# Cross-attention with absorbed queries: remainders one step later, and another order of the prologue

## What is computed

```python
x = x + xattn(layernorm(x), ctx_768, Wq, Wk, Wv, Wo, bo)   # 16 heads of 64, no mask
x = x + attn(layernorm(x), wq, wk, wv, wo)                 # causal, 16 heads of 64
x = x + ffn(layernorm(x), router, gate, up, down)          # 8 experts, top 2, silu
```

```python
q = layernorm(x) @ Wq;  k = ctx @ Wk;  v = ctx @ Wv
out = softmax(q @ k.T * 64 ** -0.5) @ v;  x + concat(out) @ Wo + bo
```

## Time and profile before

| | us |
|---|---|
| median of 3 runs | 2505.78 (2503.46 to 2507.37) |
| the profiled execution | 2506.52 |
| its span | 2504.8 |
| PE busy in the span | 2282.4 (91%) |
| DVE busy | 1612.8 (64%) |
| ACT busy | 1273.0 (51%) |
| POOL busy | 833.2 (33%) |

### The profile page before, as it was taken

How to read it: one execution, slowest core, us unless ns; L and a number is a source line. 1 busy time by engine, 2 the same in 40 slices (tenths; PEclk the granted TensorE clock), 3 DMA queues, 4 the chain that set the end, 5 groups by cost and what they waited for, 6 DMA issues and landing times. The chain is left out here.

```text
span 2504.8 us, 56060 instructions
## 1 busy us (share of the span) xinstructions
PE 2282.4 (91%) x18992; PEld 2030.0 (81%) x18992; DVE 1612.8 (64%) x3655; ACT 1273.0 (51%) x3906; POOL 833.2 (33%) x1022
## 2 busy tenths in 40 slices
PE   6999999999999999989999699999999984999996
PEld 6878888888788878878888589999999972788885
DVE  5656655665666666656655488988988857444442
ACT  4444444444444444444444377667666641444442
POOL 2323322332232323232322222222222230677674
PEclk8999999999999999999999899999999985999998
DMA  3000000000000000000000400000000011333434
GB/s 99 26 18 11 23 17 25 8 25 17 25 8 25 17 25 8 25 17 13 21 13 5 144 1 19 17 8 17 17 8 17 18 43 32 97 77 76 102 52 101
DMA packets 61946, 82.52 MB, mean 33 GB/s; under 512 B 9936, under 2 KB 45520, under 8 KB 61808
## 3 DMA queue, kind: packets, MB, share of 16 engines
q1 hardware_dynamic: 48912, 63.46, 7.9%
q0 software_dynamic: 12960, 18.12, 4.3%
HBM read 59.80 MB, written 25.96 MB: 34 GB/s over the span
## 5 line engine op out<-in xcount | busy, mean ns | idle before, releaser
L401 POOL TENSOR_TENSOR p_sb<-p_sb,rinv 128x512 f32<-128x512 f32 x256 | 266.8, 1042 | 933.6 <-DVE rinv L741 933.6
L652 ACT ACTIVATE p_sb<-s_ps,nmax 128x256 f32<-128x256 f32 x512 | 238.4, 471 | 603.1 <-DVE nmax L724 566.2
L907 POOL TENSOR_TENSOR sp_sb<-sp_sb,srinv 128x512 f32<-128x512 f32 x128 | 133.4, 1042 | 424.9 <-DVE srinv L1101 424.9
L58 DVE SCALAR_TENSOR_TENSOR q_sb<-m_ps,q_sb 64x256 fp32r<-64x256 f32 x256 | 108.1, 422 | 218.3 <-ACT q_sb L46 216.4
L65 PE MATMUL s_ps<-cx_hi,qk_hi 128*128 128x256 f32 x512 | 170.1, 332 | 41.5 <-DVE qk_hi L57 39.2
L1049 ACT ACTIVATE sp_sb<-sm_sb,snmax 128x128 f32<-128x128 f32 x512 | 199.4, 390 | 7.2 <-DVE snmax L1112 4.1
L724 DVE TENSOR_REDUCE nmax<-s_ps 128x2 f32<-128x512 f32 x256 | 175.1, 684 | 30.7 <-PE s_ps L65 30.3
L45 ACT CAST qk_hi<-qk_ps 128x512 fp32r<-128x512 f32 x248 | 148.0, 597 | 75.9 <-PE qk_ps L65 75.9
L57 DVE TENSOR_TENSOR qk_lo<-qk_ps,qk_hi 128x256 fp32r<-128x256 f32 x248 | 105.4, 425 | 121.5 <-ACT qk_hi L45 116.8
L749 DVE COPY pt_sb<-t_ps 128x512 f32<-128x512 f32 x256 | 177.0, 691 | 8.3 <-PE t_ps L544 0.8
L544 PE MATMUL t_ps<-ident,p_sb 128*128 128x128 f32 x1024 | 156.0, 275 | 7.7 <-DVE pt_sb L749 2.3
(11 more groups left out here) (293 smaller groups left out, 7644.2 us busy)
## 6 DMA issues: line engine op xcount, KB each, us to landing
ctx_raw<-in_ctx_t SPq DMA_DIRECT2D x32, 256.0 KB, 2.8
ctx_raw<-in_ctx_t SPq DMA_DIRECT2D x64, 128.0 KB, 2.9
x_ring<-in_x SPq DMA_DIRECT2D x16, 256.0 KB, 2.8
x_mid<-x_ring SPq DMA_DIRECT2D x16, 256.0 KB, 2.2
xn<-f_xn SPq DMA_DIRECT2D x16, 256.0 KB, 2.2
acc<-x_sb SPq DMA_DIRECT2D x16, 256.0 KB, 2.3
e_raw<-in_gate SPq DMA_DIRECT2D x8, 512.0 KB, 3.9
e_raw<-in_up SPq DMA_DIRECT2D x8, 512.0 KB, 4.9
```

What stands on the lines that cost most here:

```text
L58: return nc.vector.scalar_tensor_tensor(out=lo, in0=src, scalar=scale, in1=f32(hi), op0=ALU.mult, op1=ALU.subtract)
L401: nc.gpsimd.tensor_tensor(prob, prob, inv, ALU.mult).then_inc(norm_done, 1)
L652: ex = nc.scalar.activation(p_sb[:, k, b * J:(b + 1) * J], s_ps[1 - w][:, b * J:(b + 1) * J], ACT.Exp, bias=nmax[:, k, b:b + 1], scale=1.0 ...
L907: nc.gpsimd.tensor_tensor(prob, prob, inv, ALU.mult).then_inc(norm_done, 1)
```

## The change

The units and projections of the middle groups are dealt out anew. In the odd tile step 1 and step 3 now have an early and a late unit, so that units 0 to 8 are made there, and 9 to 15 in steps 0 to 6 of the even tile; step 7 of the even tile has none. Projections go to steps 0, 1, 2, 4, 6 of the odd tile and 0, 2, 4 of the even one. The remainder of a late unit is no longer taken in its own step but in the next one, right behind the maximum. ACT rounds the projection (and in the first tile the late unit and the turned keys) ahead of the exponentials. DVE copies `pt_sb` ahead of the reciprocal. In the prologue five pairs of keys are turned ahead of the split of Wq instead of two behind it on ACT and DVE, and the identity products have 16 moving columns instead of 64.

```diff
-            EARLY_WK, WARM = 3, 24
+            EARLY_WK, WARM = 5, 24
+            ODD_PROJ, EVEN_PROJ = {0: 0, 1: 1, 2: 2, 4: 3, 6: 4}, {0: 5, 2: 6, 4: 7}
+            ODD_UNIT = {(1, False): 0, (1, True): 1, (2, True): 2, (3, False): 3, (3, True): 4,
+                        (4, True): 5, (5, True): 6, (6, True): 7, (7, True): 8}
...
-                if u == 1 and p % 2 == 0 and look:
-                    return PAIRS * (t // 2 + 1) + p // 2, p // 2
-                if u == 0 and p % 2 == 0 and not drain:
-                    return PAIRS * (t // 2) + PAIRS // 2 + p // 2, PAIRS // 2 + p // 2
+                if u == 1 and look and p in ODD_PROJ:
+                    return PAIRS * (t // 2 + 1) + ODD_PROJ[p], ODD_PROJ[p]
+                if u == 0 and not drain and p in EVEN_PROJ:
+                    return PAIRS * (t // 2) + EVEN_PROJ[p], EVEN_PROJ[p]
...
             def absorption(t, u, p, first, look, drain, late):
-                m = PAIRS * (t // 2)
                 if first:
                     return p, p, int(late), 0
-                if u == 1 and p and late and look:
-                    pair = (p - 1) // 2
-                    return m + PAIRS + pair, pair, (p - 1) % 2, PAIRS * t + 1 + pair
-                if u == 0 and not drain and (late or p == PAIRS - 1):
-                    i = PAIRS - 1 + p + (p == PAIRS - 1 and late)
-                    return m + i // 2, i // 2, i % 2, PAIRS * t - PAIRS + 1 + i // 2
+                if u == 1 and look and (p, late) in ODD_UNIT:
+                    i = ODD_UNIT[p, late]
+                    return PAIRS * (t // 2 + 1) + i // 2, i // 2, i % 2, PAIRS * t + 1 + i // 2
+                if u == 0 and not drain and late and p < PAIRS - 1:
+                    i = PAIRS + 1 + p
+                    return PAIRS * (t // 2) + i // 2, i // 2, i % 2, PAIRS * t - PAIRS + 1 + i // 2
                 return None
+
+            def unit_behind(t, u, p, first, look, drain):
+                if first or drain:
+                    return None
+                if p:
+                    return absorption(t, u, p - 1, False, look, False, True)
+                return absorption(t - 1, 1, PAIRS - 1, False, True, False, True) if u == 0 else None
...
# PE, prologue
-                    pe.matmul(y_ps[:, 0:HEAD], ident[:], ident[:, 0:HEAD], start=True, stop=True)
+                    pe.matmul(y_ps[:, 0:16], ident[:], ident[:, 0:16], start=True, stop=True)
...
# ACT, tile: these lines now stand ahead of the exponentials instead of behind them
+                        if first:
+                            absorbed_hi(*late, two_banks=True)
+                            if EARLY_WK + p < PAIRS:
+                                wk_hi_copy(EARLY_WK + p)
+                        if proj is not None:
+                            q_hi(*proj)
...
# ACT and DVE, prologue: wk_hi_copy and wk_lo_copy of pairs 1 and up ahead of the split of Wq
+                for pair in range(1, EARLY_WK):
+                    wk_hi_copy(pair)
                 for n in range(Q_SPLIT):
                     weights.split_hi(act, n)
-                for pair in range(1, EARLY_WK):
-                    wk_hi_copy(pair)
...
# DVE, tile
+                        behind = unit_behind(t, u, p, first, look, drain)
...
                             (maximum)
+                        if behind is not None:
+                            absorbed_lo(*behind[:3], two_banks=False)
...
-                        if (not first if p < LAG_S else cur):
-                            dve.wait_ge(exp_done, n)
-                            nc.vector.reciprocal(rinv[:, (p - 1) % 4, :], rsum[:, (p - 1) % 4, :]).then_inc(rinv_done, 1)
-                        if late is not None and not first:
-                            absorbed_lo(*late[:3], two_banks=False)
...
                             (copy of pt_sb)
+                        if (not first if p < LAG_S else cur):
+                            dve.wait_ge(exp_done, n)
+                            nc.vector.reciprocal(rinv[:, (p - 1) % 4, :], rsum[:, (p - 1) % 4, :]).then_inc(rinv_done, 1)
```

More of the change, by code:

```diff
@@ L655, in tile @@
                             ex.then_inc(exp_done, 1)
-                        if first:
-                            absorbed_hi(*late, two_banks=True)
-                            if EARLY_WK + p < PAIRS:
-                                wk_hi_copy(EARLY_WK + p)
-                        if proj is not None:
-                            q_hi(*proj)
                         if first:
@@ L784, in _ @@
                 xt_lo_copy(0)
+                for pair in range(1, EARLY_WK):
+                    wk_lo_copy(pair)
                 for n in range(Q_SPLIT):
                     weights.split_lo(dve, n)
-                for pair in range(1, EARLY_WK):
-                    wk_lo_copy(pair)
                 q_lo(0, 0)
```

## The result

| | before | after |
|---|---|---|
| median, us (lowest to highest of 4 runs) | 2506.57 (2503.46 to 2507.56) | 2469.16 (2464.55 to 2471.37) |
| ratio after to before, 95% interval | | 0.985 (0.9833 to 0.9868) |
| span of the profiled execution, us | 2504.8 | 2462.8 |
| a steady group, us | 85.38 | 83.03 |
| first projection starts at, us | 19.18 | 22.10 |

The forecast was 2480 with a range of 2457 to 2501: right in sign and inside the range, 11 us too high. The 42.0 us between the two spans divide as follows: 14 groups 31.9, the last group 0.7, prologue and first tile together 5.65, drain and start of the next phase 2.6, all behind it 1.2. The code behind it is the same in every kernel here and takes 1088 us (after) to 1097 us (rinv_first) in the traces, and the profiled execution of the kernel after is the lowest of its four: by the medians the difference is 37.4 us.

The account below looks back on a forecast made before the run. TensorE's own order was taken to bound the kernel. Steady groups 20 us, prologue and first tile 6 and drain 1.1 summed to 27 us less than 2506.5, about 2480, with a range of 2457 to 2501.

Parts of the forecast that it names:

- What bounds the kernel: From 84 to 1400 us TensorE, busy 1218.6 of 1316 us, sets the pace; its 97 us idle can be won.
- I therefore take all 10.9 as gone: In each steady group, 10.9 us of waits, lower clock and small delays would all go.
- What comes: In each steady group, new waits of units for the remainder behind the next maximum, 9.5 us in all.
- the path from scores to unit: From the scores' end of issue through maximum and two subtractions back to PE: 1.83 us.
- charges for covered steps: In a group's six steps with a projection, where the wait is just covered: 0.02 us charged for each.
- The change doesn't do what it says: Rival: the remainder comes 0.25 us later than worked out in seven steps of each group; 2503 us, chance 0.05.
- First tile and prologue: -6: Before the steady groups: first tile 9 us less, first projection 3 us later, net 6 us gained.
- Narrow identity products at nothing: In the prologue, 16 moving columns save nothing: the stationary operand sets the distance and the products stay 10.5 us long.
- the warm products do get shorter: Rival: the prologue's identity products end sooner and the first turn starts 3 us earlier; 2477 us, chance 0.11.
- Drain -1.1: At the drain DVE copies `pt_sb` ahead of a waiting reciprocal, so the last transposes come 1.1 us earlier.
- The new waits are smaller: Rival: remainders come in time and each group wins 1.6 us more; 2458 us, chance 0.08.
- The chance of 0.17 for a fall of the clock: Two rivals: the clock falls once a group (2501 us, chance 0.10) or at two places (2522 us, chance 0.07).

Follow-up runs that it names:

- rinv_first: The kernel after with DVE's reciprocal ahead of the copy of `pt_sb` again: 2473.64 us, 0.9879 of the kernel before.
- deal_only: The kernel after, but steady groups keep only the new deal of units and projections, with orders and remainders as before: 2482.29 us, 0.9909 of the kernel before.
- own_step: The kernel after with the remainder of a late unit taken in its own step again: 2445.73 us, 0.9739 of the kernel before.
- order_only: The kernel after with the old deal and remainders in their own step, keeping ACT's and DVE's new orders and the new prologue: 2438.12 us, 0.9738 of before.
- exp_first: The kernel after with the exponentials ahead of `q_hi` again in the steady groups: 2504.47 us, 0.999 of the kernel before.
- held: The kernel after with DVE waiting for its own maximum before the remainder behind it: 2509.74 us, 1.0004 of the kernel before.
- ln_in_y: The kernel after with late units behind transposes, odd step 3's second unit in step 4, layernorm in even step 4: 2367.53 us, 0.9453 of before.
- early3: The kernel after with three early turned pairs and the split of Wq ahead of pairs 1 and 2 again: 2470.04 us, 0.9842 of before.
- warm64: The kernel after with 64 moving columns in the identity products again: 2469.01 us, 0.9858 of the kernel before.

## Why the prediction was right, step by step

**What bounds the kernel: right.** TensorE's own order sets the pace. Every run moved by what its group lost or gained in front of TensorE.

**"I therefore take all 10.9 as gone": right in the sum, its reason only in part.** The waits of the earlier trace rows and the slow stretch did go. But the prediction gave the values' wait to DVE's queue, where the late remainder held up the maximum. deal_only and own_step show that this is not the only way to lose it: both keep the remainder in its own step, and the values' wait is 40.1 us in the one and 17.3 in the other, which differ in the orders only (`q_hi` against exponentials on ACT, reciprocal against remainder on DVE). order_only has 18.4. The orders remove more than half of that wait; in the kernel after the rest is gone as well, at the price of the later remainder. And with the later remainder none of it is left even under ACT's old order (exp_first), so the prediction's way works too; what it left out is that the orders do most of it without the new waits. For the scores' wait at step 7 it is the deal, as predicted: deal_only has no such wait. But the orders alone end the slow stretch as well, though 1.71 us of that wait stay. (The prediction's 3.97 for a step stands in no row, give 4.01; nothing hangs on it.)

**"What comes", the new waits: right in place and cause; the path from scores to unit 0.11 us too long.** Loss over a step without waits, in us:

| place | forecast | measured |
|---|---|---|
| odd tile, step 3 | 2.63 | 2.52 |
| odd tile, step 5 | 0.78 | 0.61 |
| odd tile, step 7 | 1.22 | 0.87 |
| even tile, step 1 | 1.68 | 1.52 |
| even tile, step 3 | 1.43 | 1.72 |
| even tile, step 5 | 0.78 | 0.60 |
| even tile, step 6 | 0.78 | 0.66 |
| charges for covered steps, rounding | 0.2 | 0.0 |
| sum | 9.5 | 8.5 |

This is the mis-sized term. From the end of issue of the scores to the unit the prediction had 1.83; the timeline above gives 510.01 - 508.29 = 1.72 (508.29 is 0.11 behind the start of the last scores' matmul). 0.02 of the 0.11 is addition: the prediction's terms make 1.81. The other 0.09 is the maximum: the prediction added 0.683 for it and 0.02, and the row shows 0.61 from its start to the remainder's, since DVE starts this subtraction before the maximum has ended. held puts a wait there, gets 0.91, and pays 2.47 us a group: the gain of the change hangs on this distance, though held prices 0.30 us of it and not the 0.09 that the forecast had wrong. The odd tile's step 7 is 0.35 off, because `cr_lo` holds the maximum up by 0.22 and not by 0.44 (it starts 532.29 - 531.87 = 0.42 behind the end of issue of the scores, 0.20 at step 3). The other places are off by 0.11 to 0.18, of which up to 0.07 stays without a cause. 9.5 - 8.5 is the 1 us by which a group gained more than forecast (2.35 for 1.4), and it makes 12 (31.9 for 20) of the 15 us by which the forecast missed the profiled difference (42 for 27). The last group, which I gave nothing, is 0.7 of the others, and start and rest of the later phases, not in the forecast, are some 2.7; 1.2 of these lie in code that the change doesn't touch and are chance. ("The change doesn't do what it says" adds up to 2504 or 2505, not 2503.)

The Trainium skill bears on both. By "VectorE: DVE Perf Modes", section "Two Vector instructions with no wait between them", only a held instruction starts when all before it have finished, and the trace agrees: 0.61 behind the start of 0.69. Its section "The DRAIN you can't avoid" says that a semaphore behind each instruction costs nothing extra. That is no contradiction to held: the maximum signals its semaphore in both kernels, and what costs 0.30 us (0.91 for 0.61) is that the next instruction waits for it.

**The even tile's step 3, the one that was longer.** The layernorm's application takes 1.44 us, not the 0.92 of before, and it now lies beside POOL's multiplication:

```profile
551.14 0.17 DVE L760 RECIPROCAL rinv<-rsum 128x2 f32<-128x2 f32 x1
551.22 1.44 DVE L184 TENSOR_SCALAR ln_xn_x<-x_ring,ln_mv_x,ln_rstd_x 128x256 f32 x2
551.38 1.13 POOL L411 TENSOR_TENSOR p_sb<-p_sb,rinv 128x512 f32<-128x512 f32 x1 [3.23 <-DVE rinv L760]
```

The runs give this length at four overlaps with POOL's work. In ln_in_y nothing of POOL runs beside it, and it takes 0.74; before, `cr_hi` lies beside it for 0.45 us, and it takes 0.92; after, multiplication and `cr_hi` for 1.32, and 1.44; in rinv_first for 1.47, and 1.57:

```profile
521.45 0.74 DVE L184 TENSOR_SCALAR ln_xn_x<-x_ring,ln_mv_x,ln_rstd_x 128x256 f32 x2 [0.82 <-POOL ln_rstd_x L177]
```

```profile
550.67 1.57 DVE L184 TENSOR_SCALAR ln_xn_x<-x_ring,ln_mv_x,ln_rstd_x 128x256 f32 x2
551.00 1.09 POOL L51 TENSOR_TENSOR cr_hi<-ctx_raw,zero 128x512 fp32r<-128x512 f32 x1
```

(The first block is ln_in_y, the second rinv_first.) So the length goes with the overlap, by about half of it. It is not the move of the reciprocal that brings the overlap, since rinv_first has undone it and is no shorter.

**First tile and prologue: -6, measured -5.65; prologue +3, measured +2.9.** early3 shows that the five early pairs are not what gains. By exclusion what gains is the order in the first tile; that was not run alone. That the sum is met to 0.4 us is in part luck: with this prologue and first tile the odd tile's scores start at 77.0 to 78.8 us in the traces, which would be -7.0 to -5.2, and the granted clock rises and falls at other times in each of them.

**Narrow identity products at nothing: right.** warm64 settles the rival "the warm products do get shorter": 10.51 and 10.43. The LDWEIGHTS rule of the Trainium skill's page "TensorE: Matmul & The Clock Gate" would have had them end at 6.8 us; they end at 12.1 and 12.2. But the reading of the distance of 0.213 us in the prediction, that it is simply how long this instruction takes, is wrong. It is a matter of the clock. In the first tile of the kernel after, the same kind of product (128 stationary, 128 moving columns, four in a row) is recorded at both levels, the first where the granted clock is 0.50 and the second where it is 1.00:

```profile
38.12 1.05 PE L490 MATMUL o_ps<-ident,ctx_raw 128*128 128x128 f32 x4
...
44.50 0.60 PE L490 MATMUL o_ps<-ident,ctx_raw 128*128 128x128 f32 x4
```

```profile
38.00:39.50 1.50, 1.50 (x9) 1.50 (x9) 0.71 (x3) 0.87 (x2) 0.00 (x0) 0.50 0.00 0
44.00:45.50 1.50, 1.50 (x15) 1.50 (x14) 1.44 (x4) 1.04 (x3) 0.83 (x1) 1.00 0.00 0
```

They are 0.21 us apart ((1.05 - 0.42) / 3) at the lower level and 0.11 at the upper one ((0.60 - 0.28) / 3). So the trace agrees with the 107 ns of the Trainium skill where the clock is up, and the identity products, 0.21 apart, ran at the lower level. The 1.00 that the profile prints for 2 to 10 us is no measurement: the trace's first record of the clock starts at 17.2 us (14.5 in the kernel before), and a time without a record counts as full clock. What warm64 shows, that 16 and 64 moving columns take the same time, holds for the lower level; no run has these products at the upper one.

**Drain -1.1: right for the wait.** The last transposes wait 1.03 instead of 2.3; rinv_first gives the 2.30 back. The drain as a whole is 2.6 shorter; the kernel before has a slow stretch in it (granted clock 0.57 from 1400 to 1404 us), the kernel after has none.

**The rivals.** "The new waits are smaller" was the nearest to what happened, in mechanism too, at 0.08; it stood at 1.6 us a group, and 1.0 came. The clock did not fall in the groups: 1.00 from 84 to 1359 us, though in the stretch behind the longest wait TensorE is busy no more than in exp_first ahead of its fall:

```profile
508.00:512.00 4.00, 2.34 (x13) 1.58 (x12) 2.28 (x7) 1.30 (x5) 2.04 (x2) 1.00 0.00 0
```

What separates this place from that of exp_first (2.35 of 4, and 0.57 behind it) stays open, so that no fall came is in part luck. The chance of 0.17 for a fall of the clock was not too high. The row that spoke against it, 1.58 of 4 at a clock of 1.00, was one of two alike: from 50 to 54 us in the same tile TensorE is busy 1.66 of 4, and from 55.5 to 58.9 the clock is lower. "The change doesn't do what it says" was wrong as put (the remainder is no later than worked out), but half right in another way: the edit of its name is the part that costs most.

**What wasn't tried.** The later remainder under the old deal: the odd tile's first scores need unit 15, whose remainder would then stand behind the maximum of those same scores, and neither could start. ACT's order and DVE's order each by itself under the old deal, and the first tile's order by itself, were not run either.

## What to carry to other kernels

Before moving a release behind a longer instruction, write down how much work the waiting engine has between the two: here the wait cost nothing where TensorE had 1.88 us and 0.6 to 0.9 where it had 1.16, and moving four transposes in front of it was worth more than the whole change. When a change has several edits, time each order and each deal by itself and then together, since they may win the same wait: deal and orders gave 1.6 and 4.4 us a group alone and 4.0 together, and 1.4 of each was the same slow stretch. A queue in which an instruction that others wait for stands behind one that nobody waits for soon (exponentials ahead of `q_hi`) is the first thing to look for.

## What the runs showed of the hardware

- Behind a maximum of 0.69 us VectorE starts the next subtraction 0.61 after the maximum's start, 0.08 before its end; a wait on that maximum puts it 0.22 behind the end (held). Not every pair overlaps: the second subtraction, on 64 rows, starts 0.02 behind the end of the first (509.53 for 509.10 + 0.41).
- VectorE's layernorm application, 0.74 us alone, takes 0.92, 1.44 and 1.57 us with GpSimd busy beside it for 0.45, 1.32 and 1.47.
- Four float32 products in a row with 128 stationary and 128 moving columns start 0.21 us apart where the granted clock is 0.50 and 0.11 apart where it is 1.00. With 16 and with 64 moving columns they start 0.21 apart in the prologue, ahead of the first record of the clock; the 1.00 below is printed for a time without a record.
- The granted clock can fall behind 2.64 us of idle (before, in thirteen groups) and behind 1.76 (exp_first, in some groups), and stay behind 2.63 (before, in its second group), 1.56 (after, in every group) and 1.87 (held, in most groups). A fall costs 1.4 to 1.5 us of a group. The length of a single wait doesn't decide it.

The prologue's stretch of the kernel after:

```profile
2.00:10.00 8.00, 8.00 (x39) 8.00 (x39) 1.90 (x8) 0.09 (x1) 0.73 (x1) 1.00 0.94 240
```
